# Ten small mask pieces for the first row block, and four edits beside them, in a masked-attention and graph-aggregation kernel

## The reference

```python
def layernorm(x): return (x - mean(x)) / sqrt(var(x) + 1e-5)      # over the last axis

# x: 4096 x 128 float32, adj: 4096 x 4096 float32 of zeros and ones, beta: 1, weight: 128 x 128
norm2 = norm(x, axis=1, keepdims=True)
cos = beta[0] * (x @ x.T) / (norm2 @ norm2.T + 1e-07)
P = softmax(cos + (1.0 - adj) * -1e9, axis=1)
x1 = layernorm(x + P @ x)
out = layernorm(x1 + adj @ (x1 @ weight))
```

## Time and profile before

| | us |
|---|---|
| median of 3 runs | 494.19 |
| lowest and highest run | 492.16 and 495.86 |
| the profiled execution's own time | 495.08 |
| its span, from the first to the last instruction | 493.3 |
| between the two | 1.8 |
| mean granted TensorE clock over the span | 0.996 of full speed |

### The profile page before, as it was taken

One profiled execution on the slowest core, in us unless ns is written; L12 is line 12 of the kernel. 1 busy time (PEld: TensorE's weight loads), 2 busy tenths in 40 slices (PEclk: granted clock), 3 DMA queues, 4 the chain that ended last, 5 costly groups with the idle time before them and its releaser, 6 DMA issues.

```text
span 493.3 us, 8887 instructions
## 1 busy us (share of the span) xinstructions
PE 465.9 (94%) x3491; PEld 302.1 (61%) x3491; DVE 377.7 (77%) x631; ACT 316.2 (64%) x374; POOL 52.8 (11%) x65
## 2 busy tenths in 40 slices
PE   0888999999999999999999999999989999999994
PEld 0545666666666676676676666766764455554484
DVE  4988999999999999999999999999973022211253
ACT  5896987898898789889878988987861000000000
POOL 5310010210110020111102002000100000000011
PEclk9999999999999999999999999999999999999998
DMA  8989999999999999989996997960052010011111
GB/s 193 108 95 134 115 112 130 115 159 163 105 147 135 141 143 115 154 133 76 151 136 97 148 123 122 90 144 22 0 172 70 17 41 25 21 44 43 44 43 44
DMA packets 102250, 50.20 MB, mean 102 GB/s; under 512 B 70448, under 2 KB 98768, under 8 KB 102224
## 3 DMA queue, kind: packets, MB, share of 16 engines
q0 software_dynamic: 18480, 16.78, 40.8%
q1 hardware_dynamic: 83456, 33.06, 31.4%
q10 hardware_dynamic: 288, 0.07, 0.1%
HBM read 77.40 MB, written 22.82 MB: 203 GB/s over the span
## 4 chain that ended last, share of the span: by engine, by line
PE 75%; DMA 12%; DVE 5%; issue 3%; ACT 3%; POOL 1%; POOLq 0%; ACTq 0%; DVEq 0%
PE psum L979 22%; PE psum L916 18%; PE psum L920 9%; PE psum L895 8%; PE psum L894 8%; PE psum L893 8%; DMA adj_bytes<-in_adj 6%; DMA adjT<-adj_bytes 6%; DVE E L667 3%; ACT E L452 2%; PE psum L989 1%; DVE el L675 1%; DMA adjT<-in_x 1%; POOL rn L383 1%; ACT eh L461 1%
## 5 line engine op out<-in xcount | busy, mean ns | idle before, releaser
L916 PE MATMUL psum<-xaug,eh 128*128 128x257 f16 x1024 | 184.8, 274 | 7.3 <-DVE el L675 4.6
L452 ACT ACTIVATE E<-psum,sc 128x1024 f32<-128x1024 f32 x128 | 154.1, 1204 | 44.3 <-PE psum L895 43.3
L920 PE MATMUL psum<-xaug,el 128*128 128x129 f16 x1024 | 175.7, 221 | 0.0
L667 DVE SCALAR_TENSOR_TENSOR E<-E,adjT 128x1024 f32<-128x1024 f32 x128 | 156.1, 1219 | 14.6 <-ACT E L452 8.5
L675 DVE SCALAR_TENSOR_TENSOR el<-E,eh 128x1024 f16<-128x1024 f32 x128 | 155.9, 1218 | 0.0
L461 ACT ACTIVATE eh<-E 128x1024 f16<-128x1024 f32 x128 | 134.1, 1047 | 7.1 <-DVE E L667 6.7
L916 PEld LDWEIGHTS psum<-xaug,eh 128*128 128x128 f16 x1024 | 99.3, 98 | 36.6 <-DVE el L675 7.2
L979 PE MATMUL psum<-adjT,uT 128*128 128x512 fp8e4 (+1 forms) x576 | 112.1, 355 | 0.0
L920 PEld LDWEIGHTS psum<-xaug,el 128*128 128x128 f16 x1024 | 100.3, 98 | 13.1
L893 PE MATMUL psum<-uT 128*128 (+1 forms) x256 | 97.9, 382 | 1.1 <-ACT E L452 1.1
L894 PE MATMUL psum<-uT 128*128 (+1 forms) x256 | 97.6, 381 | 0.0
(11 more groups left out here) (73 smaller groups left out, 160.3 us busy)
## 6 DMA issues: line engine op xcount, KB each, us to landing
adj_bytes<-in_adj POOLq DMA_DIRECT2D x31, 512.0 KB, 11.9
adjT<-in_x SPq DMA_DIRECT2D x4, 512.0 KB, 7.0
xres<-in_x SPq DMA_DIRECT2D x8, 256.0 KB, 3.3
q_row<-norms SPq DMA_DIRECT2D x8, 256.0 KB, 7.7
x_rows<-x SPq DMA_DIRECT2D x8, 256.0 KB, 2.9
E<-x_rows SPq DMA_DIRECT2D x8, 256.0 KB, 3.0
out<-E SPq DMA_DIRECT2D x16, 128.0 KB, 2.2
x_parts<-x1p SPq DMA_DIRECT2D x7, 256.0 KB, 3.6
```

Of the source, the lines that this page charges most:

```text
L452: nc.scalar.activation(E[:, m % RING, :, :], S[m % 2], ACT.Exp, bias=col(C_BB), scale=col(C_BS)).then_inc(e_done, 1)
L667: nc.vector.scalar_tensor_tensor(out=e, in0=e, scalar=EPRE, in1=mask_bytes(b, m), op0=ALU.mult, op1=ALU.min).then_inc(masked, 1)
L916: return nc.tensor.matmul(O[t][:, 0:XC], eh[:, s, a, cols], xaug[:, j, :], start=start, stop=stop)
L920: return nc.tensor.matmul(O[t][:, 0:D + 1], el[:, s, a, cols], xaug[:, j, 0:D + 1], start=False, stop=False)
```

## The change

It has five parts.

1. **Pieces of block 0.** `FIRST` has ten pieces: f0 to f3 as before, and f4 to f9 of two pairs each in place of pieces 1 to 3 of four pairs. f4 is cast at the place of the old piece 1; f5 to f9 each wait until the piece three before has landed. Piece 4 (block 1's first) waits for f8, piece 5 for f9, and from piece 6 on the rule is the old one.
2. **The last chunk's unit rows on POOL.** Chunk 3 is scaled by eight `tensor_scalar` instructions of one tile on POOL (`unit_rows_p`), between the casts of f4 and f5, in place of one instruction over eight tiles on DVE.
3. **x's first chunk in halves.** SP loads tiles 0 to 3 and 4 to 7 with two DMAs; DVE squares tiles 0, 1, 4, 5, 6 and ACT tiles 2, 3, 7, each waiting for the second half only where it needs it.
4. **Extremes.** PE transposes group 1 of the unit rows ahead of the first transposition of the extremes; the second transposition is issued between the two halves (three matmuls each) of the first scores. DVE's four scale steps are spread among `unit_rows(2)`, `uT_lo_part(1)` and `q`.
5. **Moments.** Seven small DVE instructions per block (`combine`, `mean_var`, `variance`) become one `bn_aggr` per tile and one `tensor_scalar`. For the last half block PE adds x1 in PSUM with a product of the identity and x1 (`add_rows`), ahead of its wait for ACT's copy of the sum, and DVE reads PSUM for `bn_stats` and for the normalisation, without an addition of its own. The counts of `chain` go from 6 to 5 for each block.

```diff
-    FIRST = [(0, 1), (1, 1), (2, 1), (3, 1)]
+    FIRST = [(0, 1), (1, 1), (2, 1), (3, 1), (4, 2), (6, 2), (8, 2), (10, 2), (12, 2), (14, 2)]
...
-        mean = sb("mean", [P, 8], F32)
-        tmp = sb("tmp", [P, 3, 8], F32)
+        mv = sb("mv", [P, 8, 2], F32)
...
-        C_half = [C[1], O[1]]
+        C_half = C[1]
+        C_last = [O[1], O[2]]
...
-        SQ_V = (5, 4, 4, 4)
+
+        SQ_V = [(0, 1, 4, 5, 6)] + [range(c * CT, c * CT + CT // 2) for c in range(1, NC)]
+        SQ_A = [(2, 3, 7)] + [range(c * CT + CT // 2, (c + 1) * CT) for c in range(1, NC)]
...
 
             if c == 1:
                 engine.wait_ge(u_done_a, 1)
+            elif c == NC - 1:
+                engine.wait_ge(u_done_p, 1)
             else:
-                engine.wait_ge(u_done, (1, None, 2, 3)[c])
+                engine.wait_ge(u_done, (1, None, 2)[c])
...
             for c in range(NC):
                 half = slice(c * CT // 2, (c + 1) * CT // 2)
+                if c == 0:
+                    head = slice(0, CT // 4)
+                    sp.dma_start(rows_in_twos(xfull)[:, head, :], x_c[:, head, :]).then_inc(x_head, 16)
+                    half = slice(CT // 4, CT // 2)
                 sp.dma_start(rows_in_twos(xfull)[:, half, :], x_c[:, half, :]).then_inc(x_in[c], 16)
 
...
-            load_mask(0)
+            for f, (k, n) in enumerate(FIRST):
+                sp.wait_ge(first_cast[f], 16)
+                sp.dma_start_transpose(adjT[:, 0, k:k + n, :],
+                                       first_piece(adj8_v, f).bitcast(U16)).then_inc(first_in[f], 16)
...
-                if k == 2:
-                    pool.wait_ge(first_in[len(FIRST) - 1], 16)
-                elif k > 2:
-                    pool.wait_ge(piece_in[(k - 2) % MP], pieces_in(*divmod(k - 2, MP)))
+                if k < MP + 2:
+                    pool.wait_ge(first_in[len(FIRST) - 2 + k - MP], 16)
+                else:
+                    pool.wait_ge(piece_in[(k - 2) % MP], 16 * ((k - 2) // MP))
                 pool.dma_start(piece(adj8_v, b, c), piece(adj_v, b, c)).then_inc(piece_cast[c], 16)
 
             def cast_first(f):
+
+                if f > 4:
+                    pool.wait_ge(first_in[f - 3], 16)
                 pool.dma_start(first_piece(adj8_v, f), first_piece(adj_v, f)).then_inc(first_cast[f], 16)
 
             def inverse_norms(c):
                 pool.wait_ge(n2_done, c + 1)
                 nc.gpsimd.tensor_tensor(rn[:, chunk(c)], n2[:, chunk(c)], half_pow[:, chunk(c)],
...
+            def unit_rows_p(c):
+                pool.wait_ge(rn_done, c + 1)
+                for t in range(c * CT, (c + 1) * CT):
+                    last = nc.gpsimd.tensor_scalar(work[:, t, :], xfull[:, t, :], rn[:, t:t + 1], USC, ALU.mult, ALU.mult)
+                last.then_inc(u_done_p, 1)
...
             inverse_norms(2)
             inverse_norms(3)
-            for k in range(1, 2 * MP + 2):
+            cast_first(4)
+            unit_rows_p(NC - 1)
+            for f in range(5, len(FIRST)):
+                cast_first(f)
+            for k in range(MP, 2 * MP + 2):
                 cast(k)
             def power(done, o, n):
...
-                act.wait_ge(x_in[c], 16)
-                for t in range(c * CT + SQ_V[c], (c + 1) * CT):
+                if c == 0:
+                    act.wait_ge(x_head, 16)
+                else:
+                    act.wait_ge(x_in[c], 16)
+                for t in SQ_A[c]:
+                    if t == CT - 1:
+                        act.wait_ge(x_in[0], 16)
...
-            def scales():
-
+            px = col(C_PX).bitcast(I32)
+
+            def tiny_norms():
                 dve.wait_ge(rows_turned, 1)
                 nc.vector.tensor_copy(sc[:, C_G0:C_G1 + 1], rows_turn[:, 0:2]).then_inc(maxima, 1)
                 dve.wait_ge(maxima, 1)
                 nc.vector.tensor_scalar(flag[:, :], col(C_G1), -2.0, None, ALU.is_gt).then_inc(flag_set, 1)
-                px = col(C_PX).bitcast(I32)
                 nc.vector.tensor_scalar(px, col(C_G0).bitcast(I32), 0x7F800000, 1, ALU.bitwise_and,
                                         ALU.logical_shift_right).then_inc(xs_step, 1)
-                dve.wait_ge(xs_step, 1)
-                nc.vector.tensor_scalar(px, px, float(127 << 22), None, ALU.add).then_inc(xs_step, 1)
                 dve.wait_ge(flag_set, 1)
                 nc.vector.tensor_copy(col(C_T2), flag[:, :]).then_inc(scaled, 1)
-                dve.wait_ge(xs_step, 2)
-                nc.vector.tensor_scalar(px, px, 0x7F800000, None, ALU.bitwise_and).then_inc(xs_step, 1)
-                dve.wait_ge(xs_step, 3)
-                nc.vector.tensor_scalar_mul(col(C_XI), col(C_PX), 2.0 ** -14).then_inc(xs_step, 1)
-                dve.wait_ge(xs_step, 4)
-                nc.vector.reciprocal(col(C_XS), col(C_XI)).then_inc(xs_step, 1)
+
+            def scale_step(n):
+
+                dve.wait_ge(xs_step, n)
+                if n == 1:
+                    nc.vector.tensor_scalar(px, px, float(127 << 22), None, ALU.add).then_inc(xs_step, 1)
+                if n == 2:
+                    nc.vector.tensor_scalar(px, px, 0x7F800000, None, ALU.bitwise_and).then_inc(xs_step, 1)
+                if n == 3:
+                    nc.vector.tensor_scalar_mul(col(C_XI), col(C_PX), 2.0 ** -14).then_inc(xs_step, 1)
+                if n == 4:
+                    nc.vector.reciprocal(col(C_XS), col(C_XI)).then_inc(xs_step, 1)
...
-            scales()
+            tiny_norms()
             unit_rows(2)
+            scale_step(1)
             uT_lo_part(1)
+            scale_step(2)
             dve.wait_ge(rn_done, NC)
             nc.vector.reciprocal(q[:, :], rn[:, :]).then_inc(norms, 1)
-            unit_rows(3)
+            scale_step(3)
+            scale_step(4)
...
-                if not later(b) and m < len(FIRST):
-                    dve.wait_ge(first_in[m], 16)
-                elif m == 0:
-                    dve.wait_ge(piece_in[0], 16 * b)
+                if not later(b):
+                    for f, (k, _) in enumerate(FIRST):
+                        if k == m:
+                            dve.wait_ge(first_in[f], 16)
                 elif m % (NP // MP) == 0:
-                    dve.wait_ge(piece_in[m // (NP // MP)], 16 * (b + 1))
+                    dve.wait_ge(piece_in[m // (NP // MP)], 16 * b)
...
+            def mean_var(o, n=IT, order=chain):
+                for t in range(o, o + n):
+                    last = nc.vector.bn_aggr(mv[:, t, :], stats[:, t, :])
+                last.then_inc(order, 1)
+
+            def variance(o, base, n=IT, order=chain, scale=1.0):
                 dve.wait_ge(order, base + 2)
-                nc.vector.tensor_scalar(tmp[:, 2, s_], tmp[:, 2, s_], scale / D, scale_eps(scale), ALU.mult, ALU.add)
-                nc.vector.scalar_tensor_tensor(out=tmp[:, 1, s_], in0=tmp[:, 1, s_], scalar=0.25 * scale,
-                                               in1=tmp[:, 1, s_], op0=ALU.mult, op1=ALU.mult)
...
+                if half == 0:
+                    nc.vector.tensor_tensor(st[:, 0:HT, D:2 * D], C_half[:, 0:HB].rearrange("p (t d) -> p t d", d=D),
+                                            st[:, 0:HT, 0:D], ALU.add).then_inc(last_rows, 1)
+                    dve.wait_ge(last_rows, 1)
+
+                def src(t):
+                    return st[:, t, D:2 * D] if t < HT else C_last[t - HT][:, 0:D]
+
                 for t in ts:
-                    last = nc.vector.bn_stats(stats[:, IT + t, :], st[:, t, D:2 * D])
+                    last = nc.vector.bn_stats(stats[:, IT + t, :], src(t))
                 last.then_inc(last_rows, 1)
-                combine(IT + half * HT, base + 1, HT, last_rows)
-                mean_var(IT + half * HT, base + 1, HT, last_rows)
-                variance(IT + half * HT, base + 1, HT, last_rows)
+                dve.wait_ge(last_rows, (base if half else base + 1) + 1)
+                mean_var(IT + half * HT, HT, last_rows)
+                variance(IT + half * HT, base if half else base + 1, HT, last_rows)
                 dve.wait_ge(rstd_done, 2 * NB + half)
-                normalise_rows(1, ts)
+                normalise_rows(1, ts, src)
...
             turn_unit_rows(0)
+            turn_unit_rows(1)
             pe.wait_ge(ext_step, 3)
             nc.tensor.transpose(ext_turn, ext[:, :], ident[:, :]).then_inc(ext_turned, 1)
-            turn_unit_rows(1)
-            pe.wait_ge(ext_spread, 1)
-            nc.tensor.transpose(rows_turn, ext_rows[:, :], ident[0:NT, 0:NT]).then_inc(rows_turned, 1)
+
+            def turn_extremes():
+                pe.wait_ge(ext_spread, 1)
+                nc.tensor.transpose(rows_turn, ext_rows[:, :], ident[0:NT, 0:NT]).then_inc(rows_turned, 1)
 
             def scores(b, m):
...
                     last = nc.tensor.matmul(o, lj, hi, start=False, stop=True)
+                    if not later(b) and m == 0 and a == 0:
+                        turn_extremes()
...
```

(47 more changed lines are left out.)

52 lines of the change are left out of this document (15 added, 37 removed).

## The result

The changed kernel takes 492.47 us (median of 20 runs, 490.54 to 495.22) against 494.75 (median of 20 runs, 492.16 to 497.31) for the kernel before: ratio 0.9954, 95% interval 0.9936 to 0.9971. That is 2.3 us faster, where 1.9 were forecast. The profiled execution took 492.14 us with a span of 490.3, 3.0 us less than the one before.

The account below looks back on a forecast made before the run. PE was taken to bound most of the span, with DVE waiting for the mask's supply in block 0 and a serial end. Gains of 1.2 (head) and 0.7 (end) made 1.9 us: 492.3 us, own range 491.0 to 494.0, overall 488.4 to 496.8.

Parts of the forecast that it names:

- What bounds, and the demand: Steady stretch: PE bounds; block 0: DVE waits 4.98 us for masks. Without them block 1's pair 0 comes at 62.7.
- Part 1: Block 0's smaller mask pieces: waits at pairs 4 and 8 go, piece 4 lands at 66.7, 1.2 us earlier.
- The link of two pairs: Cast plus transposition of a two-pair piece: 13.4 us, between 10.6 for one pair and 19.0 for four.
- SP's work ahead of piece 4's transposition: SP's queue: three added transpositions, xres, norms store and q_row done near 53, before piece 4's cast lands near 58.
- The bound by packet prices: DMA casts: two-pair packets at 0.108 us, piece 4 landing at 70.4; rival of dearer transfers, 1.8 us slower, 496.0, chance 0.27.
- fixed cost of each DMA: Skill's rule, about 2.0 us per DMA: six more transfers 12 us, over three chains 4 us, time near 497.5.
- Part 2: Unit rows on POOL: 0.35 us per instruction, 2.8 for eight; up to 0.71 each PE does not wait.
- Part 3: x's first chunk in halves at the start: gain taken as 0, between -0.6 and +0.3 us.
- Part 4, and the 0.3 us of parts 2 to 4: Start, pair 0: first scores from 13.75, not 14.54; 0.3 us won for these parts, bounds 0 and 0.9.
- Part 5: Moments at the kernel's end: fewer small DVE instructions and no addition win 0.7 us, bounds 0.3 and 1.0.
- Piece 4 in time: Rival at the head: links of 11.5 us or less, gain 6.0 us, 488.2; chance 0.18.
- Slow POOL: Rival at the start: POOL's unit-row instructions at 1.67 us each, 3.9 us slower, 498.1; chance 0.08.

Follow-up runs that it names:

- e7: e4 with four small pieces under way in place of three (f waits for f - 4); 490.20 us.
- e1: The kernel before with only the small pieces of block 0 and their casts' waits; 493.81 us, ratio 0.9974.
- e6: e4 with piece 4, block 1's first, also in pieces of two pairs; 490.39 us.
- e10: Changed kernel with four small pieces under way, piece 4 in halves, unit rows behind f5's cast, and DVE's low part of group 1 behind the scale steps; 489.93 us.
- e4: Changed kernel with chunk 3's unit rows back on DVE as one instruction behind the scale steps; 491.25 us.
- e8: e4 with block 0 in sixteen pieces of one pair, as many bytes under way; 490.53 us.
- e5: Changed kernel with two more unused powers on POOL between the unit rows and f5's cast; 496.85 us, ratio 1.0045.
- e9: e7 with the extremes as before: second transposition ahead of the first scores, scale steps in one run; 489.74 us.
- e3: Changed kernel with the norms' store behind f4's transposition, and first xres load, store wait and q_row load behind those of pieces 4 and 5; 494.42 us.
- e12: e9 with the norms' store behind f5's transposition, and first xres load, store wait and q_row load behind those of pieces 4 and 5; 489.66 us.

## Why the prediction was right

The time was forecast from two gains, at the head and at the end, and both came. The head's size came out of several errors that partly cancel, and the chain that it was worked out from was not the one that ended last. The profiled runs differ by 3.0 us of span (2.2 and 0.8), more than the 1.9 forecast; that the medians differ by 2.3, and that the forecast time of 492.3 stands 0.2 from the measured one, is in part luck: it started from a median of three runs, 494.19, where twenty give 494.75.

**What bounds, and the demand.** Right. With no mask late, pair 0 of block 1 starts at 63.3 (e7), where 62.7 was worked out; the 0.6 between them go back to the first mask, which was put too early (part 4 below).

**Part 1.** In outline the mechanism was right: the waits in block 0 went, and the one for piece 4 grew. The link of two pairs was put at 13.4 us, a third of the way between one and four pairs. The six small links took 11.6, 11.5, 14.2, 13.2, 13.2 and 11.6 us, 12.6 on average. f5 was cast at 20.52, not 19.6, and f5 and f8 took 24.7 in place of 26.8, so piece 4's cast came at 45.79 for 46.4. Its own link was 19.9 for 20.3. In sum pair 0 came 2.2 us earlier where the forecast had 1.2. By e1, which has this part alone, it was 1.1, and there the gain didn't come by f5 and f8 at all, as piece 4 was cast at 47.82, no earlier than before: it came by piece 4's own link, 19.0 us.

One step of it was wrong: that SP's work ahead of piece 4's transposition would be done near 53, and so cost nothing. The store took 9.8 us, where it had taken 4.2 before, and SP was free at 57.2. The cast landed at 56.6, not near 58. So the last to end was f9's cast, the store and `q_row`, by 0.6 us, and not the chain f5, f8, piece 4. That is small in the changed kernel, but it is the limit for whoever casts piece 4 earlier still, as in e6 and e10.

The bound by packet prices was too high: in the window 26 to 36 us the changed kernel's cast queue reads

```profile
q0 software_dynamic: 1064, 0.53, 64.6%
```

which is 0.646 x 10 x 16 / 1064 = 0.097 us for a packet of two pairs, where the line gave 0.108; two of them cost 0.194, as much as one of four pairs (0.191). But such a quotient is no fixed price: in the same window it is 0.140 for the same packets in e4 (1009 packets, 88.3%), which was the faster kernel, and 0.076 for one-pair packets in e8. So it says little of when a piece lands.

The rule of the Trainium skill on a fixed cost of each DMA ("DMA: Bandwidth & Descriptors", Anatomy of one DMA) would have made six more transfers 4 us dearer, by the estimate in the prediction. A fixed part is in the rows: two pairs take 12.6 us where four take 19.0. But here it went beside other transfers: e8 has twelve more DMAs than e4, with as many bytes under way, and was no slower. That rule's price for the whole kernel is not what these runs show.

**Part 2.** The term was mis-sized: 3.96 / 8 = 0.50 us for one instruction, not 0.35, still under the 0.71 from which PE would wait. That nothing else waits was wrong: the 3.96 us stand ahead of f5's cast, and e5 shows that more of POOL's time there passes to the end of the kernel (for 3.9 added, 4.4 us lost in the medians and 3.5 in the profiles, 0.7 of the latter by the clock). e4, without the 3.96, has a median 1.2 us lower.

**Part 3.** `unit_rows(0)` started at 9.04 in place of 9.26, inside the bounds given. Neither this part nor part 5 was tried by itself; part 5 is read from the rows of the end.

**Part 4, and the 0.3 us of parts 2 to 4.** This step failed. The first mask came 0.27 us later, not 0.3 earlier. The scores did what was forecast: the first exponential started at 16.76, 0.65 earlier than the 17.41 of before. But the 0.7 us that DVE waits longer (it was 0.86) were set against the 1.16 of work taken away, but 0.91 of that went to the reading of the flag, which had been covered by the instruction removed (e10), and the scores' earlier end helps no one while DVE comes after them (e9).

**Part 5.** 0.8 us for the 0.7 forecast: two `bn_aggr` took 0.25 us together, and the seven small instructions' 0.92 became 486.24 - 485.71 = 0.53; the normalisation from PSUM takes 0.73 in place of 0.60.

**The rivals.** Piece 4 in time: not in the changed kernel, but e6 and e7 reach it in their profiles, with medians 4.4 and 4.6 us under before rather than 6.0, as the start is 0.6 us late and PE has its own bound close behind. Slow POOL did not happen; e5, with POOL 3.9 us longer, is slower than before (ratio 1.0045).

## What to carry to other kernels

Follow a supply by its links (a cast and a transposition, from issue to landing) and ask of each gate how many links lie between it and the first late consumer; then add one more transfer under way before making transfers smaller or moving work. Then follow the queue that issues the last transfer too: in an in-order queue a small store with a wait behind it can end later than the transfer that was being watched, as here by 0.6 us, and making the watched one earlier then brings nothing until that store is out of the way. Look at the spread beside the median: e4 and e7 differ by 1 us in their medians and by 1.6 in their spreads (1.88 and 0.28), and e6's good median hides four late runs in twelve. An instruction that seems to count only by its length may be the cover for a register read and a branch: before removing it from the front of a loop, look at what the sequencer does there.

## What was not expected

- A store of 16 KB took 4.2 us from issue to landing beside the casts in the kernel before, and 7.0 (e8) to 10.2 (e1) at the same place of the queue in the others; moved, it took 10.5 in e3 and 5.7 in e12.
- In e8 the DMA engines had a share of 1.57 from 26 to 36 us, where the changed kernel had 1.24, and the kernel lost nothing by it: a share over 1 says little of how much room is left.
- PE's granted clock fell to 0.57 for four microseconds after four in which PE was busy 1.06 us (e5), and to 0.63 after four in which it was busy 2.46 (e1). In e3 it stayed at 1.00 after four with 1.54. What decides between them these rows don't show.
